# Two groups of x in one load, with rows of 32 KB into two slots side by side

## The chip, the cores and the metric

The kernel runs on one core of one Trainium2 chip. The metric is the device time of one execution in microseconds, the median of several runs. Times inside the kernel come from one profiled execution and count from the start of its span.

## The reference

The model is a factorization machine with a small network on top, for a batch of 1024 rows with 12,500 features each, all in float32. With x of shape 1024 x 12500, factors of 12500 x 16 and one linear weight per feature:

```
x_reg = x @ W_lin.T + b_lin
emb   = x @ factors                                    # 1024 x 16
sum_squared = square(emb.sum(axis=1))
squared_sum = (square(x) @ square(factors)).sum(axis=1)
h   = relu(emb @ W1.T + b1)                            # 16 -> 128
h   = relu(h @ W2.T + b2)                              # 128 -> 64
dnn = h @ W3.T + b3
y   = 0.5 + 5 * sigmoid(x_reg + 0.5 * (sum_squared - squared_sum) + dnn)
```

Nearly all of the data is x, 51.2 MB. Every element is read once, multiplied by 17 weights, and its square by one more.

## The kernel before

The host transposes x, so that features lie on the 128 partitions and the batch on the free axis. 12,500 features are one chunk of 128 (`xf`), a rest of 84 (`xl`), and 96 more chunks. The batch is worked in two halves of 512 columns. In a half, eight chunks make a group: 128 partitions x 8 chunks x 512 columns, 2 MB, in which each partition's row is 16 KB. There are 12 groups of the first half and 8 of the second; the last 32 chunks of the second half come apart, as ten "end pieces" of x that are cut by columns into a block of 384 and one of 128 (`PIECES`), so that the layers of the first block can run while the last loads still come.

**Ring.** `xr` has four slots (`RING`) of one group each, and so has `sq`, which takes the squares. SP issues all loads on one queue, in order: the weights (`hd`, L199), `xf`, `xl`, then groups 0 to 3 into slots 0 to 3 (L202, L203). In a loop (L205 to L211) it then waits for each slot until the group in it has been used (`sq_used`, L208) and loads the next group into it (L209). The end pieces follow in the same way (L213 to L217), each as soon as the slots that it covers are free.

**Who waits for a landing.** Each slot has its own semaphore, `x_landed[s]`. Three engines wait for it, each in its own order: ScalarE squares five chunks of the group in two instructions (L260 to L267), VectorE squares three (L346 to L350), TensorE multiplies.

**TensorE.** For every group, `multiply` (L440) adds 8 products of weights and x into the bank `p_lin` of the half, and `add_squares` (L446) adds 8 products of the squares, after waiting for VectorE and for ScalarE's first instruction, and before the last two for ScalarE's second. Each product shows as two records, so a group is two blocks of 16. All products are recorded on one line, L409. The last product of a group raises `sq_used` by one (L456). GpSimd sets out the weights of a group into `wr` and `wz` once the slot's last group has been used (`place`, L237).

**Between the halves.** After the 12 groups of the first half TensorE, ScalarE and VectorE run the layers of that half (L297 to L304, L359 to L362, L528 to L536), in the order of each engine's program, before any of them turns to the first group of the second half. The loads go on meanwhile, as far as slots are free. At the end the layers of the second half's two blocks are woven by hand between the end pieces (L543 to L579).

Of the kernel before, what the change touches and what calls it, by code (L numbers as in the profile page):

```python
# [14 lines left out]
P = 128  # L15
# [8 lines left out]
HALF = B // 2  # L24
CHUNKS = 8
RING = 4
ENDS = 32
ALL = (N - REST) // P
GROUPS = (ALL - 1) // CHUNKS
END_GROUPS = ENDS // CHUNKS  # L30
TOTAL = 2 * GROUPS - END_GROUPS
ROUNDS = (GROUPS // RING, (GROUPS - END_GROUPS) // RING)
W_END = ALL - ENDS

assert GROUPS % RING == 0 and (ALL - 1) % CHUNKS == 0 and END_GROUPS == RING


BY_DVE = 3
# [28 lines left out]
def fm_kernel(nc, head, x_first, x_rest, x_groups, x_end, out):  # L67
    with ExitStack() as ctx:
        def sb(name, shape, dt=F32):
            return ctx.enter_context(nc.sbuf_tensor(name, shape, dt))  # L70
# [4 lines left out]
        def sem(name):  # L75
            return ctx.enter_context(nc.semaphore(name))
# [3 lines left out]
        xl = sb("xl", [P, B])  # L80
        xr = sb("xr", [P, RING, CHUNKS, HALF])
        sqf = sb("sqf", [P, B])
        sql = sb("sql", [P, B])
        sq = sb("sq", [P, RING, CHUNKS, HALF])
        fsq = sb("fsq", [P, ALL, EMB])
        fsql = sb("fsql", [P, EMB])
        s_all = sb("s_all", [P, ALL])
        wr = sb("wr", [P, RING, CHUNKS, LIN])
        wz = sb("wz", [P, RING, CHUNKS, WZ])

        ws = sb("ws", [P, ENDS + 2, WZ])
        bias = sb("bias", [P, 1])
# [21 lines left out]
        hd_landed = sem("hd_landed")  # L114
        first_landed = sem("first_landed")
        rest_landed = sem("rest_landed")
        x_landed = [sem(f"x_landed{s}") for s in range(RING)]
        end_landed = [sem(f"end_landed{i}") for i in range(len(PIECES))]
        y_stored = sem("y_stored")
        zero_set = sem("zero_set")  # L120
# [11 lines left out]
        sq_used = sem("sq_used")  # L132
# [24 lines left out]
        def cols(k):  # L157

            c, n = BLOCKS[k]
            return slice(c, c + n)  # L160
# [6 lines left out]
        def row(k):  # L167

            c, n = BLOCKS[k]
            return slice(c // 2, (c + n) // 2)  # L170

        def tot_bank(k):
            return p_tot[k % 2]

        def width(i):
            return BLOCKS[PIECES[i][0]][1]

        def piece(a, i, c, n):

            at = ENDS * (BLOCKS[PIECES[i][0]][0] - HALF)  # L180
            return a[:, at + c * width(i):at + (c + n) * width(i)]
# [5 lines left out]
        def last_slot(i):  # L187
            k, c, n, _ = PIECES[i]
            return (ENDS * (BLOCKS[k][0] - HALF) + (c + n) * BLOCKS[k][1] - 1) // (CHUNKS * HALF)

# [6 lines left out]
        @block.sync  # L197
        def _(sp):
            sp.dma_start(hd[:, :], head).then_inc(hd_landed, 16)  # L199
            sp.dma_start(xf[:, :], x_first).then_inc(first_landed, 16)  # L200
            sp.dma_start(xl[0:REST, :], x_rest).then_inc(rest_landed, 16)  # L201
            for s in range(RING):  # L202
                sp.dma_start(xr[:, s].rearrange("p c b -> p (c b)"), x_groups[s]).then_inc(x_landed[s], 16)  # L203

            with sp.Fori(1, sum(ROUNDS)) as r:  # L205
                for s in range(RING):

                    sp.wait_ge(sq_used, RING * r + s + 1)  # L208
                    sp.dma_start(xr[:, s].rearrange("p c b -> p (c b)"),  # L209
                                 x_groups[bass.ds(RING * r + s, 1)].rearrange("g p n -> (g p) n")  # L210
                                 ).then_inc(x_landed[s], 16)  # L211
            at = 0
            for i, (k, c, n, _) in enumerate(PIECES):  # L213
                rows = x_end[at:at + P * n * width(i)].rearrange("(p m) -> p m", p=P)
                sp.wait_ge(sq_used, TOTAL + last_slot(i) + 1)
                sp.dma_start(piece(xe, i, c, n), rows).then_inc(end_landed[i], 16)
                at += P * n * width(i)  # L217

            for k in range(3):
                sp.wait_ge(y_ready[k], 1)  # L220
                sp.dma_start(out[cols(k)].rearrange("(u b) -> u b", u=2), y[64:P:32, row(k)]).then_inc(y_stored, 16)
            sp.wait_ge(y_stored, 48)

        @block.gpsimd
        def _(pool):
# [7 lines left out]
            nc.gpsimd.tensor_copy(ws[:, 0, LIN:WZ], s_all[:, 0:1]).then_inc(ws_ready, 1)  # L233
            nc.gpsimd.tensor_copy(ws[:, 1:ENDS + 1, LIN:WZ].rearrange("p c k -> p (c k)"),
                                  s_all[:, W_END:ALL]).then_inc(ws_ready, 1)
# [16 lines left out]
        @block.scalar  # L252
        def _(act):
            act.wait_ge(zero_set, 1)
            nc.scalar.activation(warm[:, :], zero[:, 0:1], ACT.Sigmoid)
            act.wait_ge(first_landed, 16)
            nc.scalar.activation(sqf[:, :], xf[:, :], ACT.Square).then_inc(first_squared, 1)  # L257

            def squares(r, s):
                act.wait_ge(x_landed[s], 16 * (r + 1))  # L260

                act.wait_ge(sq_used, RING * r + s + 1)
                c = BY_DVE
                for n in BY_ACT:
                    nc.scalar.activation(sq[:, s, c:c + n, :], xr[:, s, c:c + n, :],  # L265
                                         ACT.Square).then_inc(act_squared, 1)
                    c += n  # L267

            def square_end(i):
                k, c, n, m = PIECES[i]  # L270
                act.wait_ge(end_landed[i], 16)
                nc.scalar.activation(piece(sq_end, i, c, m), piece(xe, i, c, m),  # L272
                                     ACT.Square).then_inc(act_end_squared, 1)

            def copy_lin(k, u):
                nc.scalar.copy(lin[:, part(k, u)], p_lin[k][:, u * BLOCKS[k][1] // 2:(u + 1) * BLOCKS[k][1] // 2]  # L276
                               ).then_inc(lin_ready[k], 1)

            def layer1(k):
                act.wait_ge(p_h1_done[k], 1)  # L280
                nc.scalar.activation(h1[:, part(k, 0)], p_h1[0][:, 0:BLOCKS[k][1] // 2], ACT.Relu,
                                     bias=pr[:, C_B1:C_B1 + 1]).then_inc(h1a_ready[k], 1)

            def embedding_square(k):
                act.wait_ge(p_es_done[k], 1)
                nc.scalar.activation(gsq[0:64, row(k)], tot_bank(k)[0:64, row(k)], ACT.Square).then_inc(gsq_ready[k], 1)

            def sigmoid(k):
                act.wait_ge(p_tot_done[k], 1)
                nc.scalar.activation(sg[64:P, row(k)], tot_bank(k)[64:P, row(k)], ACT.Sigmoid,  # L290
                                     bias=bias[64:P, :]).then_inc(sg_ready[k], 1)

            with act.Fori(0, ROUNDS[0]) as r:
                for s in range(RING):
                    squares(r, s)

            act.wait_ge(sq_used, RING + GROUPS)  # L297
            copy_lin(0, 0)
            copy_lin(0, 1)
            layer1(0)  # L300
            act.wait_ge(pads_set, 3)
            embedding_square(0)
            act.wait_ge(bias_ready, 1)
            sigmoid(0)  # L304

            with act.Fori(ROUNDS[0], sum(ROUNDS)) as r:
                for s in range(RING):
                    squares(r, s)

            for i in range(6):  # L310
                square_end(i)
            act.wait_ge(p_lin_done[1], 1)
            copy_lin(1, 0)
            copy_lin(1, 1)
            layer1(1)
            nc.scalar.copy(rest[:, :], p_lin[1][:, BLOCKS[1][1]:HALF]).then_inc(rest_copied, 1)
            square_end(6)
            square_end(7)
            embedding_square(1)
            square_end(8)  # L320
            square_end(9)
            sigmoid(1)
            embedding_square(2)
            act.wait_ge(squares_done, 1)
            nc.scalar.copy(qs[:, :], p_sq[:, 0:P]).then_inc(qs_ready, 1)
            sigmoid(2)

        @block.vector
        def _(dve):
# [13 lines left out]
            nc.vector.tensor_tensor(sql[0:REST, :], xl[0:REST, :], xl[0:REST, :], ALU.mult).then_inc(rest_squared, 1)  # L343

            def squares(r, s):
                dve.wait_ge(x_landed[s], 16 * (r + 1))  # L346

                dve.wait_ge(sq_used, RING * r + s + 1)
                nc.vector.tensor_tensor(sq[:, s, 0:BY_DVE, :], xr[:, s, 0:BY_DVE, :], xr[:, s, 0:BY_DVE, :],  # L349
                                        ALU.mult).then_inc(dve_squared, 1)  # L350
# [56 lines left out]
        def _(pe):  # L407
# [30 lines left out]
                add_mm(quad(p_lin[h], 3, WZ, 0, HALF), ws[0:REST, ENDS + 1, :], sql[0:REST, half(h)])  # L438

            def multiply(r, s, h):  # L440
                pe.wait_ge(x_landed[s], 16 * (r + 1))
                pe.wait_ge(wr_ready, RING * r + s + 1)
                for c in range(CHUNKS):
                    add_mm(quad(p_lin[h], c, LIN, 0, HALF), wr[:, s, c, :], xr[:, s, c, :])
# [182 lines left out]
```

## Time and profile before

| what | us |
|---|---|
| median of three runs | 136.48 (136.37 to 136.83) |
| the profiled execution | 136.26 |
| its span, first to last instruction | 134.2 |
| TensorE busy | 105.3 |
| ScalarE busy | 64.2 |
| VectorE busy | 52.9 |
| GpSimd busy | 13.2 |
| bytes read | 52.16 MB |

Busy times are shares of one execution, and a matmul record's own time overlaps the next one's, so TensorE's busy time is longer than the work it stands for. The profile cuts the span into 40 slices and gives for each the rate of the loads in GB/s; its chain of waits goes back from the last instruction to what released each step. A landing is not a row of its own, but VectorE starts the squares of a group when it has landed, and the row says so ("<-DMA xr<-in_x_groups").

### The profile page before, as it was taken

Reading aid. Unit: us, or ns where it says so; the run is one execution under the profiler, and the core shown is the slowest. Engines: PE = TensorE matmul, PEld = TensorE weight load, DVE = VectorE, ACT = ScalarE, POOL = GpSimd, SP = SyncE. Lnnn points to the kernel's source line nnn. Section 1 sums busy time; section 2 is a strip of 40 time slices with the busy share of each in tenths; the row PEclk is TensorE's granted clock in tenths of the full one; section 3 lists DMA queues with packets and bytes.
Section 4 is the critical chain, followed back from the end, with each engine's and each line's share of the span. In section 5 each row is a group of like instructions: output and inputs, shape, how many; then the busy total and the mean of one; then the engine's idle time right before and its main releaser. Section 6 shows DMA issues by size and latency. Waiting matters only on the chain.

```text
span 134.2 us, 2683 instructions
## 1 busy us (share of the span) xinstructions
PE 105.3 (78%) x1034; PEld 28.9 (22%) x1034; DVE 52.9 (39%) x45; ACT 64.2 (48%) x67; POOL 13.2 (10%) x49
## 2 busy tenths in 40 slices
PE   6087966965976967967978969987887799779992
PEld 1022111110211111111112312211221122214780
DVE  0391451450550451352251393153254155557531
ACT  4030652560752662562473496373374374446741
POOL 5016011011011011011011001151000000000000
PEclk9999999999999999999999999999999999999999
DMA  4999999999999999999999999999999999999400
GB/s 129 406 385 435 415 440 420 435 425 420 430 430 430 420 440 420 440 410 445 415 440 420 440 420 435 415 440 420 440 415 435 401 440 429 412 397 409 180 5 1
DMA packets 4724, 52.25 MB, mean 389 GB/s; under 512 B 534, under 2 KB 666, under 8 KB 1646
## 3 DMA queue, kind: packets, MB, share of 16 engines
q1 hardware_dynamic: 4718, 52.16, 92.7%
q8 instruction: 5, 0.08, 0.3%
q14 instruction: 1, 0.01, 0.0%
HBM read 52.16 MB, written 0.00 MB: 389 GB/s over the span
## 4 chain that ended last, share of the span: by engine, by line
DMA 61%; PE 29%; DVE 3%; SPq 2%; issue 2%; ACT 1%; DVEq 0%; ACTq 0%
DMA xr<-in_x_groups 52%; PE p_lin L409 23%; DMA xr<-in_x_end 9%; PE p_tot L409 2%; PE p_h L480 2%; PE p_sq L409 1%; DVE sq L349 1%; DVE sq L355 1%; SPq L203 1%; PE p_h L504 1%; ACT sg L290 1%; SPq L201 0%; SPq L200 0%; SPq L199 0%; ACT lin L276 0%
## 5 line engine op out<-in xcount | busy, mean ns | idle before, releaser
L265 ACT ACTIVATE sq<-xr 128x1536 f32<-128x1536 f32 (+1 forms) x40 | 48.5, 1263 | 47.1 <-DMA xr<-in_x_groups 47.1
L349 DVE TENSOR_TENSOR sq<-xr 128x1536 f32<-128x1536 f32 x20 | 35.2, 1762 | 56.5 <-DMA xr<-in_x_groups 56.4
L409 PE MATMUL p_lin<-xr,wr 128*17 128x512 f32 x320 | 38.3, 595 | 16.4 <-DMA xr<-in_x_groups 16.4
L409 PE MATMUL p_lin<-sq,wz 128*18 128x512 f32 x320 | 38.4, 595 | 2.7 <-DVE sq L349 1.2
L409 PEld LDWEIGHTS p_lin<-xr,wr 128*17 128x17 f32 x320 | 8.1, 97 | 45.4 <-issue 23.0
L409 PEld LDWEIGHTS p_lin<-sq,wz 128*18 128x18 f32 x320 | 8.3, 97 | 32.4 <-ACT sq L265 19.5
L240 POOL COPY wr<-hd x20 | 5.9, 296 | 71.9 <-PE p_lin L409 71.4
L272 ACT ACTIVATE sq<-xr 128x1536 f32<-128x1536 f32 (+5 forms) x10 | 9.0, 929 | 7.6 <-DMA xr<-in_x_end 7.6
L355 DVE TENSOR_TENSOR sq<-xr 128x1536 f32<-128x1536 f32 (+3 forms) x8 | 9.2, 1156 | 7.8 <-DMA xr<-in_x_end 7.8
L409 PE MATMUL p_lin<-xr,hd 128*17 128x384 f32 (+1 forms) x128 | 8.9, 380 | 0.7 <-DMA xr<-in_x_end 0.7
L409 PE MATMUL p_lin<-sq,ws 128*18 128x384 f32 x64 | 5.9, 487 | 1.1 <-DVE sq L355 1.1
L409 PE MATMUL p_lin<-xf,hd 128*17 128x512 f32 x4 | 3.2, 961 | 3.7 <-DMA xf<-in_x_first 3.7
L242 POOL COPY wz<-s_all x20 | 5.4, 272 | 0.0
L409 PEld LDWEIGHTS p_lin<-xr,hd 128*17 128x17 f32 x128 | 3.9, 97 | 5.3 <-issue 2.7
L332 DVE SCALAR_TENSOR_TENSOR fsq<-hd 128x1552 f32<-128x1552 f32 x1 | 1.8, 1775 | 4.4 <-DMA hd<-in_head 4.4
L257 ACT ACTIVATE sqf<-xf 128x1024 f32<-128x1024 f32 x1 | 1.1, 1057 | 4.9 <-DMA xf<-in_x_first 4.9
L366 DVE TENSOR_SCALAR h<-p_h,hd 128x256 f32<-128x256 f32 (+2 forms) x3 | 1.3, 417 | 4.4 <-PE p_h L480 4.4
L409 PE MATMUL p_sq<-sq,ws 128*18 128x128 f32 x64 | 2.9, 273 | 0.0
L409 PEld LDWEIGHTS p_lin<-sq,ws 128*18 128x18 f32 x64 | 1.8, 97 | 5.0 <-ACT sq L272 3.4
L480 PE MATMUL p_h<-lin,hd 128*32 128x256 f32 (+2 forms) x40 | 2.4, 344 | 0.5 <-ACT lin L276 0.5
L409 PE MATMUL p_lin<-xl,hd 84*17 84x512 f32 x4 | 2.6, 780 | 0.0
L290 ACT ACTIVATE sg<-p_tot,bias 64x256 f32<-64x256 f32 (+2 forms) x3 | 1.2, 397 | 2.7 <-PE p_tot L409 2.7
(49 smaller groups left out, 34.2 us busy)
## 6 DMA issues: line engine op xcount, KB each, us to landing
xr<-in_x_groups SPq DMA_DIRECT2D x20, 2048.0 KB, 15.4
xr<-in_x_end SPq DMA_DIRECT2D x3, 1536.0 KB, 13.1
xr<-in_x_end SPq DMA_DIRECT2D x3, 512.0 KB, 13.0
xr<-in_x_end SPq DMA_DIRECT2D x1, 1152.0 KB, 14.3
hd<-in_head SPq DMA_DIRECT2D x1, 934.0 KB, 4.8
xr<-in_x_end SPq DMA_DIRECT2D x2, 384.0 KB, 14.5
xf<-in_x_first SPq DMA_DIRECT2D x1, 512.0 KB, 5.9
xl<-in_x_rest SPq DMA_DIRECT2D x1, 336.0 KB
```

Source lines behind the costliest of these rows:

```text
L203: sp.dma_start(xr[:, s].rearrange("p c b -> p (c b)"), x_groups[s]).then_inc(x_landed[s], 16)
L240: nc.gpsimd.tensor_copy(wr[:, bass.ds(s, 1), :, :].rearrange("p s c k -> p (s c) k"), w[:, bass.ds(at, CHUNKS), :]).then_inc(wr_ready, 1)
L242: nc.gpsimd.tensor_copy(wz[:, bass.ds(s, 1), :, LIN:WZ].rearrange("p s c k -> p (s c k)"), s_all[:, bass.ds(at, CHUNKS)]).then_inc(wz_read ...
L265: nc.scalar.activation(sq[:, s, c:c + n, :], xr[:, s, c:c + n, :], ACT.Square).then_inc(act_squared, 1)
L272: nc.scalar.activation(piece(sq_end, i, c, m), piece(xe, i, c, m), ACT.Square).then_inc(act_end_squared, 1)
L290: nc.scalar.activation(sg[64:P, row(k)], tot_bank(k)[64:P, row(k)], ACT.Sigmoid, bias=bias[64:P, :]).then_inc(sg_ready[k], 1)
L332: nc.vector.scalar_tensor_tensor(fsq[:, :, :], w[:, :, 0:EMB], -0.5, w[:, :, 0:EMB], ALU.mult, ALU.mult).then_inc(fsq_ready, 1)
L349: nc.vector.tensor_tensor(sq[:, s, 0:BY_DVE, :], xr[:, s, 0:BY_DVE, :], xr[:, s, 0:BY_DVE, :], ALU.mult).then_inc(dve_squared, 1)
L355: nc.vector.tensor_tensor(piece(sq_end, i, c + m, n - m), piece(xe, i, c + m, n - m), piece(xe, i, c + m, n - m), ALU.mult).then_inc(dve_e ...
L409: return nc.tensor.matmul(out, lhsT, rhs, start=False, stop=False, skip_group_check=True)
L480: mm = nc.tensor.matmul(bank[32 * t:32 * t + 32, 0:n], pr[:, C_W1 + 32 * t:C_W1 + 32 * t + 32], rhs, start=True, stop=True, skip_group_che ...
L504: mm = nc.tensor.matmul(p_h2[32 * t:32 * t + 32, row(k)], pr[:, C_W2 + t % 2 * 32:C_W2 + t % 2 * 32 + 32], h1[:, part(k, t // 2)], start=T ...
```

## The change

Groups are loaded in pairs. The host lays two groups that follow each other side by side, so that each partition has one row of 32 KB for both. A transfer brings such a pair, 4 MB, into two neighbouring slots of the ring: slots 0 and 1, or slots 2 and 3. There are two landing semaphores instead of four, one for each pair of slots. SP waits until both groups of a pair of slots have been used and then issues one load. Slots, squares, products, their order on every engine, and the end pieces stay as they were.

```diff
+TWO = 2
...
-        x_landed = [sem(f"x_landed{s}") for s in range(RING)]
+        x_landed = [sem(f"x_landed{t}") for t in range(RING // TWO)]
...
-            for s in range(RING):
-                sp.dma_start(xr[:, s].rearrange("p c b -> p (c b)"), x_groups[s]).then_inc(x_landed[s], 16)
+            for t in range(RING // TWO):
+                sp.dma_start(xr[:, TWO * t:TWO * t + TWO].rearrange("p s c b -> p (s c b)"),
+                             x_groups[t]).then_inc(x_landed[t], 16)
 
             with sp.Fori(1, sum(ROUNDS)) as r:
-                for s in range(RING):
-
-                    sp.wait_ge(sq_used, RING * r + s + 1)
-                    sp.dma_start(xr[:, s].rearrange("p c b -> p (c b)"),
-                                 x_groups[bass.ds(RING * r + s, 1)].rearrange("g p n -> (g p) n")
-                                 ).then_inc(x_landed[s], 16)
+                for t in range(RING // TWO):
+
+                    sp.wait_ge(sq_used, RING * r + TWO * t + TWO)
+                    sp.dma_start(xr[:, TWO * t:TWO * t + TWO].rearrange("p s c b -> p (s c b)"),
+                                 x_groups[bass.ds(RING // TWO * r + t, 1)].rearrange("g p n -> (g p) n")
+                                 ).then_inc(x_landed[t], 16)
...
-                act.wait_ge(x_landed[s], 16 * (r + 1))
+                act.wait_ge(x_landed[s // TWO], 16 * (r + 1))
...
-                dve.wait_ge(x_landed[s], 16 * (r + 1))
+                dve.wait_ge(x_landed[s // TWO], 16 * (r + 1))
...
-                pe.wait_ge(x_landed[s], 16 * (r + 1))
+                pe.wait_ge(x_landed[s // TWO], 16 * (r + 1))
...
-    x_groups = np.empty((TOTAL, P, CHUNKS * HALF), f32)
+    x_groups = np.empty((TOTAL // TWO, P, TWO, CHUNKS * HALF), f32)
     for g in range(TOTAL):
         h, c = g // GROUPS, CHUNKS * (g % GROUPS)
-        x_groups[g] = chunks[c:c + CHUNKS, :, h * HALF:(h + 1) * HALF].transpose(1, 0, 2).reshape(P, -1)
+        x_groups[g // TWO, :, g % TWO] = chunks[c:c + CHUNKS, :, h * HALF:(h + 1) * HALF].transpose(1, 0, 2).reshape(P, -1)
+    x_groups = x_groups.reshape(TOTAL // TWO, P, TWO * CHUNKS * HALF)
```

## Rows read from the trace of the kernel before

**Rows 1.** The page: span, load rate in 40 slices, last chain by line.
```profile
span 134.2 us, 2683 instructions
...
GB/s 129 406 385 435 415 440 420 435 425 420 430 430 430 420 440 420 440 410 445 415 440 420 440 420 435 415 440 420 440 415 435 401 440 429 412 397 409 180 5 1
...
DMA xr<-in_x_groups 52%; PE p_lin L409 23%; DMA xr<-in_x_end 9%; PE p_tot L409 2%; PE p_h L480 2%; PE p_sq L409 1%; DVE sq L349 1%; DVE sq L355 1%; SPq L203 1%; PE p_h L504 1%; ACT sg L290 1%; SPq L201 0%; SPq L200 0%; SPq L199 0%; ACT lin L276 0%
```

**Rows 2.** Timeline of VectorE: start, duration in us, instruction, count, idle before and releaser.
```profile
5.58 1.77 DVE L332 SCALAR_TENSOR_TENSOR fsq<-hd 128x1552 f32<-128x1552 f32 x1 [4.44 <-DMA hd<-in_head]
...
18.19 1.76 DVE L349 TENSOR_TENSOR sq<-xr 128x1536 f32<-128x1536 f32 x1 [3.15 <-DMA xr<-in_x_groups]
...
27.96 1.76 DVE L349 TENSOR_TENSOR sq<-xr 128x1536 f32<-128x1536 f32 x1 [3.13 <-DMA xr<-in_x_groups]
33.59 1.76 DVE L349 TENSOR_TENSOR sq<-xr 128x1536 f32<-128x1536 f32 x1 [3.87 <-DMA xr<-in_x_groups]
...
67.84 1.76 DVE L349 TENSOR_TENSOR sq<-xr 128x1536 f32<-128x1536 f32 x1 [3.13 <-DMA xr<-in_x_groups]
...
87.94 1.84 DVE L349 TENSOR_TENSOR sq<-xr 128x1536 f32<-128x1536 f32 x1 [3.64 <-DMA xr<-in_x_groups]
...
107.52 1.76 DVE L349 TENSOR_TENSOR sq<-xr 128x1536 f32<-128x1536 f32 x1 [3.13 <-DMA xr<-in_x_groups]
...
123.57 0.69 DVE L355 TENSOR_TENSOR sq<-xr 128x512 f32<-128x512 f32 x1 [0.41 <-DMA xr<-in_x_end]
124.86 0.69 DVE L355 TENSOR_TENSOR sq<-xr 128x512 f32<-128x512 f32 x1 [0.59 <-DMA xr<-in_x_end]
```

**Rows 3.** Timeline of TensorE, from group 13 to the end pieces.
```profile
80.51 1.91 PE L409 MATMUL p_lin<-xr,wr 128*17 128x512 f32 x16
82.22 1.91 PE L409 MATMUL p_lin<-sq,wz 128*18 128x512 f32 x16
...
107.52 1.91 PE L409 MATMUL p_lin<-xr,wr 128*17 128x512 f32 x16 [0.99 <-DMA xr<-in_x_groups]
109.52 1.91 PE L409 MATMUL p_lin<-sq,wz 128*18 128x512 f32 x16
111.24 1.49 PE L409 MATMUL p_lin<-xr,hd 128*17 128x384 f32 x16
...
120.47 1.49 PE L409 MATMUL p_lin<-sq,ws 128*18 128x384 f32 x16 [0.40 <-DVE sq L355]
121.76 1.49 PE L409 MATMUL p_lin<-xr,hd 128*17 128x384 f32 x16
```

**Rows 4.** Timeline of SP's issues: head, two refills, the last store.
```profile
0.75 0.39 SPq L199 DMA_DIRECT2D hd<-in_head  x1
...
71.95 0.33 SPq L209 DMA_DIRECT2D xr<-in_x_groups  x1
...
84.32 0.33 SPq L209 DMA_DIRECT2D xr<-in_x_groups  x1
...
132.29 0.47 SPq L221 DMA_DIRECT2D out_y<-y  x1
```

**Rows 5.** Windows: length, busy us of each engine, clock, DMA share, GB/s.
```profile
0.75:1.50 0.75, 0.30 (x1) 0.13 (x2) 0.27 (x1) 0.75 (x1) 0.75 (x2) 1.00 0.00 0
```

**Rows 6.** Timeline of TensorE's first products.
```profile
7.22 1.86 PE L409 MATMUL p_lin<-xf,hd 128*17 128x512 f32 x2 [3.71 <-DMA xf<-in_x_first]
...
8.88 1.06 PE L409 MATMUL p_lin<-xf,hd 128*17 128x512 f32 x1
...
10.61 0.60 PE L409 MATMUL p_lin<-sqf,ws 128*18 128x512 f32 x1
...
12.01 0.59 PE L409 MATMUL p_lin<-sql,ws 84*18 84x512 f32 x1
```

**Rows 7.** Waits: who waited for whom, us in total, times, longest.
```profile
PE p_lin L409 <- DMA xr<-in_x_groups: 16.4, 17, 1.7
```

**Rows 8.** The chain of waits where the second half begins: start, us, what.
```profile
76.78 1.77 DVE sq L349
```

More of the change, by code:

```diff
@@ L33 @@
 W_END = ALL - ENDS
-assert GROUPS % RING == 0 and (ALL - 1) % CHUNKS == 0 and END_GROUPS == RING
+assert RING % TWO == 0 and GROUPS % RING == 0 and (ALL - 1) % CHUNKS == 0 and END_GROUPS == RING
 BY_DVE = 3
```

## The prediction

> **What bounds the kernel now.** I read the page first, then the landings, then what releases a slot. On the page [rows 1] the reader is to see a kernel bound by its loads: the slices move 400 to 445 GB/s from the second to the 37th, and the chain that ended last is 52% loads of x in the first 20 groups, 9% loads of the last 32 chunks, 23% matmuls. VectorE begins the squares of a group as soon as it has landed, so its starts mark the landings [rows 2]. Between 33.59 and 67.84 seven groups land, one every 4.89 us: (67.84 - 33.59)/7. TensorE needs less than that. With work in hand it starts a block of 16 matmul records (the x half or the squares half of one group) every 1.71 us (80.51 to 82.22), so a group takes it 3.43 us; from an idle start the squares hold it up once, by 2.00 instead of 1.71 (107.52 to 109.52) [rows 3]. So TensorE idles about 1 us per group, and the queue is never empty: a slot is asked for again about 4.1 us after its group has landed (67.84 to 71.95, group 11) [rows 2, 4], while three other groups, 14.7 us of transfer, are still queued. That reserve is what the change spends.
>
> Below, "group" counts from 0 and "landing" is the start of the squares. Pair p holds groups 2p and 2p+1; before, its second group lands last, so I compare with the landings of groups 1, 3, 11, 15 and 19.
>
> **The transfers themselves (a gain).** Ten transfers of 4 MB take the place of 20 of 2 MB. What one costs beyond its bytes follows from two sizes in a full queue: 2048 KB in 4.89 us, 512 KB in 1.29 us (123.57 to 124.86) [rows 2]. The slope is 3.60 us for 1536 KB, so 2048 KB of bytes are 4.80 us and 0.09 us belong to the transfer and its 128 rows. Halving transfers and rows saves 0.09 per pair: X = 9.78 - 0.09 = 9.69 us, 0.9 us over ten pairs. No row shows 32 KB rows. The lower bound is no gain (rows cut in two by the queue); the upper bound is the best slice, 445 GB/s [rows 1], by which 4.19 MB take 9.43 us. I take 9.69, next to the measured sizes. SP issues ten fewer transfers, 0.33 us each for those in the loop [rows 4], in time in which it otherwise waits for a slot: nothing.
>
> By the Trainium skill, DMA: Bandwidth & Descriptors, section "Anatomy of one DMA", a transfer costs some 2.0 us plus its bytes at 436 GB/s (a fit for another issue path). Paid in a row, that would make ten fewer transfers worth 20 us. The rows contradict it for a full queue: 2048 KB would take 6.8 us and take 4.89.
>
> **The turn of a pair (a loss of reserve).** Both slots are now released together, so after a landing TensorE does two groups before the refill is issued: 4.11 (one group, 67.84 to 71.95) plus 3.43 = 7.54 us [rows 2 to 4]. In that time only one other pair, 9.69 us, feeds the queue. The refill must reach the engines in time. An issue on an empty queue costs F beyond its bytes. The only such load is the first: head is issued at 0.75, seen at 5.58, and its 934 KB are worth 934/2048 x 4.89 = 2.23 us, so F = 2.60 [rows 2, 4]. From below: no byte moves between 0.75 and 1.50 [rows 5], so F is at least 0.75. In between: the last store of 0.5 KB, issued at 132.29, ends with the span at 134.2, 1.9 us [rows 1, 4]. I take F = 2.0, since the first load of the program also has the first read in it. The rule for each pair is then: landing = the later of (landing of the pair before + X) and (issue + F + X). Steady state: 7.54 + 2.0 = 9.54 against 9.69: just no stall. At F = 2.6 there is one of 0.45 us in every second pair.
>
> **First pair.** Group 0 alone no longer starts the work; pair 0 lands at 18.19 - 0.09 = 18.10 instead of 13.28. The lost start is itself hidden, since the loads go on. But TensorE, which ended its first matmuls at 12.6 (12.01 + 0.59), stands still for 5.5 us [rows 6]. Since its clock rose it had never stood longer than 1.7 us for a landing [rows 7]. Rows 6 show what a pause does at the start: after the clearing matmuls it waited 3.71 us, and the first products then took 1.06 us a record where the same shape later takes 0.60, the lower level (1.2 GHz) against the upper (2.4 GHz). (The clock column reads 1.00 even at the start [rows 5], so I go by the durations.) It ran 2.7 us (7.22 to about 9.9) before it was on the upper level. I expect pair 0 to start on the lower level and to lose half of such a stretch, 1.35 us. Bounds: 0 (the clock holds) and 6.8 us (all four blocks of both groups at half speed, 4 x 1.71 more). Then: issue at 18.10 + 7.54 + 1.35 = 26.99, landing of pair 2 at 26.99 + 2.0 + 9.69 = 38.68; without a stall 18.10 + 2 x 9.69 = 37.48. Cost 1.20 us, on the path, since everything behind is loads. After that the gaps are some 2.5 us (9.69 less two groups' 7.2), nearer to the 1.7 that the clock outlasted, and I cost them at nothing. (The extra 0.74 us before 33.59 is in the old trace and I leave it in both.)
>
> The Trainium skill has this rule in TensorE: Matmul & The Clock Gate, section "HAM oscillation — how this bites in real kernels": bursts of matmuls with a wait for loads between them can fall back to the lower clock each time. The trace shows no fall in gaps up to 1.7 us, so for the shorter waits the measurement stands against it; at the long first gap the page and rows 6 point the same way.
>
> **The middle, where half 0 ends.** After group 11 TensorE, ScalarE and VectorE do the layers of the first half; VectorE is back at squares at 76.78 [rows 8]. Before, that delay ate reserve only: the slot of group 13 was reissued at 84.32 [rows 4], with two more groups still on their way. Now (without the first stall) pair 5 lands at 67.84 - 6 x 0.09 = 67.30, its refill is issued at 74.84, 2.89 us later than group 11's at 71.95, and the layers and groups 12 and 13 follow 2.89 later: refill at 84.32 + 2.89 = 87.21. Pair 7, the last one queued, lands at 87.94 - 8 x 0.09 = 87.22. So pair 8 lands not at 87.22 + 9.69 = 96.91 but at 87.21 + 2.0 + 9.69 = 98.90, a stall of 1.99 us. Pair 9 (issued around 95, in time) lands at 108.59; group 19 landed at 107.52. Net +1.07: stall 1.99, less 0.92 saved.
>
> **The end.** Groups 18 and 19 now reach TensorE together, and it has no gap left before the end. From a landing: 3.72 for group 18 (107.52 to 111.24), 3.43 for group 19, four blocks of 1.29 for the end pieces 0 and 1 (120.47 to 121.76), and 1.29 for the x half of piece 2 [rows 3]: the squares of piece 2 start 13.60 after the landing, at 122.19, where they started at 120.47: +1.72. VectorE's 1.76 us per square and the last loads, which move by +1.07, are both earlier than that. From 120.47 on TensorE had work without a gap, so the rest moves as a whole.
>
> **Sum** against the profiled execution (136.26 us; span 134.2): +1.72 and +1.20, 139.18. The median of the runs, 136.48, lies 0.22 higher, so 139.4.
>
> **Rivals.**
> - A, the sum above: 139.4. Chance 0.42.
> - B, the clock holds in the first gap: the first refill at 25.64 is in time (25.64 + 11.69 = 37.33 before 37.48), and only the middle costs: 138.2. For it: the upper level never fell in 120 us of the old trace; against it: no gap there was half as long. 0.25.
> - C, an empty queue costs F = 2.6 each time: 0.6 more in the middle and 0.45 at pairs 2, 4 and 6, thus 140.2 with the clock up, 141.5 with A's slow first pair. For it: the only measured load from empty; against it: that one also opens the program. 0.17.
> - D, the other side: long rows stream so much faster that they pay for the stalls. Each 0.1 us less of X brings the end forward by about 0.8. With B's clock it decides at X = 9.47 (443 GB/s); at 9.43, the best slice, it gives 138.2 - 2.1 = 136.1. Against it: the stretch between 33.59 and 67.84 runs at 429 and the fitted cost of 0.09 leaves no more to save. 0.08.
> - E, rows cut in two, so the change saves nothing: A plus about 0.7, 140.1. 0.08.
>
> Range: 137.6 (B with F = 1.4) to 141.6 (C at its worse end), which leaves out D and little else. A measurement of this kernel can tell about 0.3%, 0.4 us, from no change; D splits evenly between faster and same, so faster 0.04, same 0.04, slower 0.92.
>
> **What would show it.** Right: landings 9.7 us apart in pairs, two groups back to back on TensorE and a gap of about 2.5 us; a first landing near 18.1; products of pair 0 at some 1 us a record at first; a hole in the load rate near 28 and one near 88 to 89; pair 9 near 109.8 (108.6 without the first stall); TensorE without gaps from there on. Wrong: no hole near 88 (then the release in the middle came earlier than I place it), holes in every pair (C), pair 0 at 0.60 us a record (B), pairs closer than 9.6 us (D) or 9.8 apart with as many packets as before (E).

## The result, and the profile after

The changed kernel takes 147.71 us (median of four runs, 147.31 to 149.29) against 136.55 before: 1.084 times as long (95% interval 1.080 to 1.087). Forecast was 139.4. The direction was right and the size was not: 11.2 us lost, 2.9 expected. Times and ratios, here and below, leave out executions that took over 1.5% longer than the fastest of the same kernel.

The page after, with lines that answer to [rows 1]: the span, the granted clock of TensorE in tenths and the load rate, each in 40 slices; the last chain; and its line on the loads (count, KB each, us from issue to landing).
```profile
span 145.2 us, 2649 instructions
...
PEclk9999857999659999959999999968959999999999
...
GB/s 154 433 367 433 433 433 433 131 406 433 433 433 433 244 361 433 433 433 433 289 388 433 406 433 433 221 424 433 289 397 433 380 435 261 387 396 417 235 5 1
...
DMA xr<-in_x_groups 51%; PE p_lin L412 41%; PE p_sq L412 1%; PE p_tot L412 1%; PE p_h L483 1%; SPq L203 0%; SPq L202 0%; SPq L201 0%; PE p_h L507 0%; ACT sg L293 0%; SPq L212 0%; ACT gsq L289 0%; DVE y L379 0%
...
xr<-in_x_groups SPq DMA_DIRECT2D x10, 4096.0 KB, 14.3
```
The chain that ended last has 41% matmuls where it had 23%: the loads now wait for TensorE's work. In undisturbed slices the loads run at 433 GB/s, a little better than before. But the row has a hole every third to sixth slice (131, 244, 289, 221, 289, 261), and the clock falls beside several of them. The landings show the holes, VectorE's timeline as in [rows 2]:
```profile
18.17 3.43 DVE L352 TENSOR_TENSOR sq<-xr 128x1536 f32<-128x1536 f32 x2 [7.66 <-DMA xr<-in_x_groups]
27.87 3.52 DVE L352 TENSOR_TENSOR sq<-xr 128x1536 f32<-128x1536 f32 x2 [6.28 <-DMA xr<-in_x_groups]
40.55 3.43 DVE L352 TENSOR_TENSOR sq<-xr 128x1536 f32<-128x1536 f32 x2 [9.16 <-DMA xr<-in_x_groups]
50.25 3.43 DVE L352 TENSOR_TENSOR sq<-xr 128x1536 f32<-128x1536 f32 x2 [6.27 <-DMA xr<-in_x_groups]
62.08 3.43 DVE L352 TENSOR_TENSOR sq<-xr 128x1536 f32<-128x1536 f32 x2 [8.40 <-DMA xr<-in_x_groups]
71.78 3.43 DVE L352 TENSOR_TENSOR sq<-xr 128x1536 f32<-128x1536 f32 x2 [6.27 <-DMA xr<-in_x_groups]
...
84.15 3.43 DVE L352 TENSOR_TENSOR sq<-xr 128x1536 f32<-128x1536 f32 x2
94.13 3.43 DVE L352 TENSOR_TENSOR sq<-xr 128x1536 f32<-128x1536 f32 x2 [6.55 <-DMA xr<-in_x_groups]
105.42 3.43 DVE L352 TENSOR_TENSOR sq<-xr 128x1536 f32<-128x1536 f32 x2 [7.87 <-DMA xr<-in_x_groups]
117.94 3.43 DVE L352 TENSOR_TENSOR sq<-xr 128x1536 f32<-128x1536 f32 x2 [9.09 <-DMA xr<-in_x_groups]
```
These are pairs 0 to 9. Undisturbed, a pair takes 9.70 us (18.17 to 27.87, 40.55 to 50.25, 62.08 to 71.78); forecast 9.69. Every other interval is longer: pair 2 by 2.98, pair 4 by 2.13, pairs 6 and 7 together by 2.95 (71.78 to 94.13; pair 6's row shows the layers' end, not its landing), pair 8 by 1.59, pair 9 by 2.82: 12.5 us. SP's issues of pairs 2, 4 and 9 show how late they were asked for:
```profile
28.20 0.35 SPq L212 DMA_DIRECT2D xr<-in_x_groups  x1
...
49.64 0.33 SPq L212 DMA_DIRECT2D xr<-in_x_groups  x1
...
103.10 0.33 SPq L212 DMA_DIRECT2D xr<-in_x_groups  x1
```
Call the time from a refill's issue to the landing of the pair ahead of it what is *left*. Pair 2 was issued with nothing left (28.20, pair 1 landed at 27.87), pair 4 with 0.61, pair 9 with 2.32 (pair 8 landed at 105.42) and still lost 2.82. Pairs 3 and 5, issued at 35.42 and 57.80 with 5.13 and 4.28 left, lost nothing.

TensorE's timeline of pair 0, the counterpart of [rows 3], and the windows (length, busy us of each engine, clock, loads) over the starts of pairs 0, 2 and 4:
```profile
18.17 3.62 PE L412 MATMUL p_lin<-xr,wr 128*17 128x512 f32 x16 [5.58 <-DMA xr<-in_x_groups]
21.56 2.99 PE L412 MATMUL p_lin<-sq,wz 128*18 128x512 f32 x16
24.37 1.89 PE L412 MATMUL p_lin<-xr,wr 128*17 128x512 f32 x16
26.09 1.89 PE L412 MATMUL p_lin<-sq,wz 128*18 128x512 f32 x16
```
```profile
18.00:24.00 6.00, 5.83 (x32) 1.28 (x36) 3.43 (x2) 4.75 (x4) 0.00 (x0) 0.52 1.00 431
40.00:44.00 4.00, 3.44 (x20) 0.74 (x24) 3.43 (x2) 3.46 (x3) 0.00 (x0) 0.50 0.95 410
62.00:65.00 3.00, 2.92 (x16) 0.68 (x20) 2.92 (x2) 2.93 (x3) 0.00 (x0) 0.55 1.07 459
```
After the idle 5.58 us the clock is at its lower level (0.52 over the stretch): the first two blocks take 3.39 and 2.81 us from start to next start, instead of 1.72. The same is seen behind the holes ahead of pairs 2 and 4. So two suspects stand side by side: late refills, and a clock that falls in the holes and makes the next refill later.

The packets of the loads add a third. A pair is 128 packets of 32 KB, one for each row, on 16 DMA engines, and 16 packets of 4 bytes, one behind the last row of each engine; I take these as the ends of the engines' shares. The line on packets, for six stretches of the changed kernel's trace: 102.90 to 103.65 and 104.75 to 105.10 (ends of pair 8), 104.05 to 104.75 and 106.65 to 106.98 (first rows of pair 9), 114.20 to 115.10 and 115.10 to 117.60 (ends of pair 9, among rows of the end pieces):
```profile
DMA packets 15, 0.00 MB, mean 0 GB/s; under 512 B 15, under 2 KB 15, under 8 KB 15
DMA packets 1, 0.00 MB, mean 0 GB/s; under 512 B 1, under 2 KB 1, under 8 KB 1
...
DMA packets 15, 0.49 MB, mean 702 GB/s; under 512 B 0, under 2 KB 0, under 8 KB 0
DMA packets 1, 0.03 MB, mean 99 GB/s; under 512 B 0, under 2 KB 0, under 8 KB 0
...
DMA packets 40, 0.33 MB, mean 364 GB/s; under 512 B 15, under 2 KB 15, under 8 KB 15
DMA packets 85, 1.05 MB, mean 421 GB/s; under 512 B 1, under 2 KB 1, under 8 KB 1
```
Fifteen engines had ended pair 8 by 103.62 and the last at 105.04; fifteen began pair 9 between 104.07 and 104.73, some 1.0 us and more after its issue, and the last at 106.89. That engine ended pair 9 at 117.49, the others by 115.08. The landing is the last engine's: when the refill of pair 9 was issued with 2.32 us left, fifteen of sixteen had at most some 0.5 us of work.

### The profile page after: what moved, and what is told of

It is laid out like the page before. It is cut to its first block, busy times and chain, and to the rows that moved or that the text cites. A ratio compares the mean times of both kernels' runs of the same rounds, so it can differ in the third digit from the quotient of the medians.

```text
span 145.2 us, 2649 instructions
## 1 busy us (share of the span) xinstructions
PE 109.2 (75%) x1034; PEld 32.0 (22%) x1034; DVE 52.1 (36%) x45; ACT 63.1 (43%) x67; POOL 14.4 (10%) x49
## 4 chain that ended last, share of the span: by engine, by line
DMA 51%; PE 45%; issue 1%; SPq 1%; ACT 0%; DVE 0%
DMA xr<-in_x_groups 51%; PE p_lin L412 41%; PE p_sq L412 1%; PE p_tot L412 1%; PE p_h L483 1%; SPq L203 0%; SPq L202 0%; SPq L201 0%; PE p_h L507 0%; ACT sg L293 0%; SPq L212 0%; ACT gsq L289 0%; DVE y L379 0%
## 5 line engine op out<-in xcount | busy, mean ns | idle before, releaser
L268 ACT ACTIVATE sq<-xr 128x1536 f32<-128x1536 f32 (+1 forms) x40 | 47.5, 1259 | 59.7 <-DMA xr<-in_x_groups 59.7
L412 PE MATMUL p_lin<-xr,wr 128*17 128x512 f32 x320 | 44.8, 684 | 26.5 <-DMA xr<-in_x_groups 26.5
L352 DVE TENSOR_TENSOR sq<-xr 128x1536 f32<-128x1536 f32 x20 | 34.4, 1760 | 67.6 <-DMA xr<-in_x_groups 67.5
L412 PE MATMUL p_lin<-sq,wz 128*18 128x512 f32 x320 | 40.8, 629 | 1.5 <-DVE sq L352 1.2
L412 PEld LDWEIGHTS p_lin<-xr,wr 128*17 128x17 f32 x320 | 9.2, 104 | 56.7 <-issue 52.6
L412 PEld LDWEIGHTS p_lin<-sq,wz 128*18 128x18 f32 x320 | 9.9, 106 | 32.3 <-issue 21.9
L243 POOL COPY wr<-hd x20 | 7.1, 356 | 81.7 <-PE p_lin L412 81.2
L279 ACT COPY lin<-p_lin 128x256 f32<-128x256 f32 (+1 forms) x4 | 1.2, 349 | 3.1 <-PE p_lin L412 3.1
```

What stands on the lines that cost most here:

```text
L243: nc.gpsimd.tensor_copy(wr[:, bass.ds(s, 1), :, :].rearrange("p s c k -> p (s c) k"), w[:, bass.ds(at, CHUNKS), :]).then_inc(wr_ready, 1)
L412: return nc.tensor.matmul(out, lhsT, rhs, start=False, stop=False, skip_group_check=True)
```

## The experiments

The theories: 1, the loss feeds itself through the clock, since an issue on an empty queue costs some 2.7 us and one made earlier than that costs nothing; 2, it is the loads' own (long rows, restart of an empty queue); 3, landing or release in pairs is enough by itself; 4, formed after the first four runs below (six spare products, the two halves of the change, rows of 16 KB), a refill needs far more time in hand than 2.7 us. Times stand beside runs of the kernel before on the same chip, 136.45 to 136.66 us.

**Spare work for TensorE, so that the clock holds.** Nothing else changes:
```diff
+            idle_work(16)      # spare bf16 products of 512 columns into p_h1[0]
...
+                    if s % TWO == 0:
+                        idle_work(6)
                     multiply(r, s, 0)
```


> The changed kernel with idle work for TensorE: 16 spare products of 512 columns into a bank that is free (1.2 GHz or 2.4 GHz, nothing reads them) ahead of the first pair, and six ahead of every pair, so that no pause is long enough for the clock to fall. Theory 1 (the refill is too late by a little, and each hole lets the clock fall, which makes the next refill later still): every pair is released 7.5 us after its landing instead of up to 10.0, holes of about 0.5 us at pairs 2, 4 and 6 and 2.7 us in the middle remain, 139.5 us (139 to 141). Theory 2 (the loss is the loads' own, in the restart of an empty queue or in rows of 32 KB): no change, 147 to 148 us.

147.96 and 149.84 us, ratio 1.089 (1.081 to 1.098): theory 1's 139.5 is refuted as far as six products held the clock. They did not hold it everywhere (mean 0.962), so a second run has twelve.

> As the run with idle work for TensorE, but with twelve spare products ahead of every pair instead of six (2.6 us), so that the clock has no pause to fall in even behind a hole. Theory 1 (late by the clock's falls): 139.5 us (139 to 142). Theory 4 (a refill has to be issued some 4.5 us before the pair ahead of it has landed, since an engine of the queue that has run empty restarts late, each at another time, and the landing waits for the last of 16; at the release 7.5 us after a landing only 2.2 us are left, so it is late with the clock up as well): 146 to 150 us, with 10.5 to 12.5 us between landings.

147.61 us, ratio 1.079 (1.076 to 1.082). The mean granted clock, VectorE's timeline of pairs 1 to 3 and SP's issues of pairs 2 and 3:
```profile
core 0: 145.6 us, clock 1.000
```
```profile
28.94 3.43 DVE L352 TENSOR_TENSOR sq<-xr 128x1536 f32<-128x1536 f32 x2 [7.46 <-DMA xr<-in_x_groups]
38.99 3.43 DVE L352 TENSOR_TENSOR sq<-xr 128x1536 f32<-128x1536 f32 x2 [6.62 <-DMA xr<-in_x_groups]
51.54 3.43 DVE L352 TENSOR_TENSOR sq<-xr 128x1536 f32<-128x1536 f32 x2 [9.13 <-DMA xr<-in_x_groups]
```
```profile
25.85 0.35 SPq L212 DMA_DIRECT2D xr<-in_x_groups  x1
36.49 0.34 SPq L212 DMA_DIRECT2D xr<-in_x_groups  x1
```
The clock stands at 1.000, yet pair 3, issued at 36.49 with 2.50 us left before pair 2's landing at 38.99, came 2.85 us late (51.54 - 38.99 - 9.70). Pair 2, with 3.09 left, lost 0.35. The falls of the clock go along with the loss, but the loss is there without them. By the packets fifteen engines had ended pair 3 by 48.60, and the last at 51.10.

Pair 1 came 1.2 us late in this run, with its load queued from the start. There too one engine ended late: fifteen by 27.22, the last at 28.34 (stretches 26.20 to 27.30 and 27.30 to 28.50). The third line, for 25.55 to 25.60, shows a packet of 16 KB of the queue that the page calls "instruction"; it starts at 25.57 and takes 1.02 us:
```profile
DMA packets 26, 0.36 MB, mean 328 GB/s; under 512 B 15, under 2 KB 15, under 8 KB 15
DMA packets 7, 0.20 MB, mean 164 GB/s; under 512 B 1, under 2 KB 1, under 8 KB 1
...
q8 instruction: 1, 0.02, 127.2%
```
A row of x that starts as it ends (26.57) takes 1.76 us instead of 1.22. The kernel before has such packets at 29.02 and 82.72, and its landings at 33.59 and 87.94 are 0.74 and 0.51 us late; the changed kernel has one at 90.89, ahead of the late pair 7. That these packets held up the engine is read from the times; no run took them out.

**One half of the change at a time.** The kernel before, with the release in pairs alone, and with the landing in pairs alone:
```diff
-                    sp.wait_ge(sq_used, RING * r + s + 1)
+                    if s % 2 == 0:
+                        sp.wait_ge(sq_used, RING * r + s + 2)
```
```diff
-                pe.wait_ge(x_landed[s], 16 * (r + 1))        # ScalarE and VectorE alike
+                pe.wait_ge(x_landed[s // 2], 32 * (r + 1))
```


> The kernel before with the release in pairs alone: SP waits until both slots of a pair are used and then issues their two loads of 2 MB back to back; four landing semaphores, so each group is still worked as it lands. Theory 1 (it is landing and release in pairs together that use up the reserve): at the second group's landing another 9.8 us of loads are queued and the refill is there after 4.1 + 2.7 = 6.8 us, so nothing is lost: 136.5 us, within 0.4. Theory 3 (the release in pairs alone empties the queue): 140 us or more.

> The kernel before with the landing in pairs alone: loads of 2 MB into single slots, each slot released by itself, but two slots share one landing semaphore and all engines wait for both. Theory 1: the first group's refill is issued 4.1 us after the pair's landing and the second's at 7.5, with 9.8 us of loads queued, so the queue never empties; the clock may fall in the first gap of 5.5 us; only the end is later, two groups there in a row: 137.2 us (136.6 to 138). Theory 3 (the work in pairs, with its pauses and falls of the clock, is enough by itself): 140 us or more.

Release alone: 136.84 us, ratio 1.003 (1.001 to 1.006). Landing alone: 137.40, 1.009 (1.005 to 1.013). Theory 3 falls. With the landing in pairs alone, VectorE's timeline of two pairs and the issues between them:
```profile
48.53 3.43 DVE L349 TENSOR_TENSOR sq<-xr 128x1536 f32<-128x1536 f32 x2 [6.36 <-DMA xr<-in_x_groups]
58.33 3.43 DVE L349 TENSOR_TENSOR sq<-xr 128x1536 f32<-128x1536 f32 x2 [6.37 <-DMA xr<-in_x_groups]
```
```profile
42.86 0.33 SPq L209 DMA_DIRECT2D xr<-in_x_groups  x1
46.28 0.33 SPq L209 DMA_DIRECT2D xr<-in_x_groups  x1
```
The first slot's refill is asked for with 5.67 us left, the second's then queues behind it, and the landings keep 9.80 us. The clock fell here as well (mean 0.949), and cost little.

**Both halves, but rows of 16 KB** (two loads of 2 MB in place of one of 4 MB; the two edits above together).

> Landing and release both in pairs, but two loads of 2 MB with rows of 16 KB in place of one of 4 MB. Theory 1: as the changed kernel, plus 0.09 us for each of the ten pairs: 148 to 149 us. Theory 2, as far as it blames the rows of 32 KB: back near 136.5 to 139 us.

148.97 and 148.99 us, where theory 1 had 148 to 149. The long rows are not to blame.

**The slots released earlier.** The changed kernel, whole; TensorE takes both groups' x products first, and raises a new semaphore once all squares are there:
```diff
-                    sp.wait_ge(sq_used, RING * r + TWO * t + TWO)
+                    sp.wait_ge(x_used, RING * r + TWO * t + TWO)
...
                     multiply(r, s, 0)
+                    multiply(r, s + 1, 0)
                     add_squares(r, s, 0)
+                    add_squares(r, s + 1, 0)     # its first product raises x_used by TWO
```


> The changed kernel, whole, with the slots released earlier: TensorE does the x half of both groups first, and a new semaphore releases the pair when the x products of both are done and ScalarE and VectorE have squared both, before the squares of the second group are multiplied; some 5.5 us after the landing instead of 7.5, so that 4.2 us are left. Theory 1 (2.7 us are enough when the clock is up): holes only behind the first pair and in the middle, 139 us (138 to 140). Theory 4 (4.5 us needed): most of the loss goes, but some 0.5 us at other pairs too, 141 us (139.5 to 143). If it stays at 146 or more, the time of the release is not the cause.

> The changed kernel, whole, with the early release (after both groups' x products and squares) and with twelve spare products ahead of every pair, ten more ahead of the first, so that the clock stays up: pairs released 5.4 us after the landing every time, 4.3 us ahead of need. Theory 4 (some 4.5 us needed, whatever the clock; the clock mattered only where it moved the release): small losses at pairs and one of 1 to 2 us in the middle, 139.5 us (138.5 to 141.5). If the pairs lose as much as in the run with the early release alone (145 us), the clock is not what was left there.

144.10 (of two executions) and, with spare work as well, 144.65 us (1.06 times as long as before). Some 3 to 3.5 us come back. Both expectations missed, theory 4's too: it had 139.5 to 143 and 138.5 to 141.5. In the second run, with 3.2 to 4.8 us left at a release, the pairs lose 0 to 1.5 us each, and in the middle, with 1.35 left (issue 89.71, landing ahead 91.06), 2.66.

**The transfers by themselves.** Both kernels with most of the square half of the 20 groups left out (VectorE squares one chunk, ScalarE two, one product of squares) and with spare work.

> The kernel before with most of the square half of the 20 groups left out (one chunk squared by VectorE and one chunk in each of ScalarE's two instructions, one product of squares per group), with six spare products for TensorE every second group to hold its clock: the loads as they are, slots free 3 us after a landing. Base for the next run: bound by the loads, 136 us (135.5 to 136.6).

> The changed kernel with the same part left out and 16 spare products ahead of every pair: pairs released some 4.2 us after the landing, 5.5 us ahead of need. What the larger transfers are worth by themselves. By the fitted 0.09 us for each pair: 0.9 us below the run before it, less 0.6 at the end for two groups in a row, so 0.3 us (0 to 0.9) faster. Theory 2 as far as it blames the rows of 32 KB: slower by 3 us or more. Theory 4: no holes, at most one of 1 us in the middle.

136.44 and 137.98 us (ratios to the whole kernel before: 0.999, 0.997 to 1.000, and 1.014, 1.008 to 1.020). I had expected the second 0.3 us faster than the first; it was 1.5 slower. Pairs are 9.71 us apart where undisturbed, so the saving per pair is real, but with 4.2 us left most of the time the pairs lose up to 0.7, and the middle 1.3; the change still doesn't pay.

**Late refills without pairs.** The kernel before, most of the square half left out, SP asking for a slot two groups later; in the second run six of eight x products are left out too:
```diff
-                    sp.wait_ge(sq_used, RING * r + s + 1)
+                    sp.wait_ge(sq_used, RING * r + s + 3)
```


> The kernel before, loads of 2 MB with rows of 16 KB, each group landing by itself, with most of the square half left out as in the base run (136.4 us); SP asks for a slot only when the group two later has been used, so that each refill is issued about 3.0 us after a landing with 1.8 us of loads left. No pairs, no rows of 32 KB, little work. Theory 1 (a refill costs 2.6 us from an empty queue and nothing if issued earlier than that): 0.75 us lost for every two loads, 142 us (140 to 143.5). Theory 4 (some 4.5 us needed): 1.5 to 2.5 us for every two loads, 148 to 156 us. Theory 2 as far as it blames the landing in pairs or the long rows: 136.5 us.

> As the run with the refills asked for two groups late, with six of the eight x products left out as well, so that the refill is issued 1.3 us after a landing with 3.5 us of loads left. Theory 1 (2.6 us are enough): nothing lost, 136.4 us (136 to 137). Theory 4: 0.5 to 1.5 us for every two loads, 140 to 148 us.

163.62 us (ratio 1.198, 1.194 to 1.201) and 158.91 (1.168, 1.160 to 1.176). Both are above what theory 4 named. In the first the products ran slower than I had assumed (mean clock 0.83), so at most 0.3 us were left, and each second load lost 3.4 to 4.0. The second has the fewest other changes in its way; VectorE's timeline of groups 3 to 9, and SP's issues of groups 4 to 9:
```profile
28.00 0.69 DVE L349 TENSOR_TENSOR sq<-xr 128x512 f32<-128x512 f32 x1 [4.19 <-DMA xr<-in_x_groups]
34.90 0.69 DVE L349 TENSOR_TENSOR sq<-xr 128x512 f32<-128x512 f32 x1 [6.21 <-DMA xr<-in_x_groups]
41.37 0.69 DVE L349 TENSOR_TENSOR sq<-xr 128x512 f32<-128x512 f32 x1 [5.77 <-DMA xr<-in_x_groups]
47.83 0.69 DVE L349 TENSOR_TENSOR sq<-xr 128x512 f32<-128x512 f32 x1 [5.76 <-DMA xr<-in_x_groups]
53.85 0.69 DVE L349 TENSOR_TENSOR sq<-xr 128x512 f32<-128x512 f32 x1 [5.33 <-DMA xr<-in_x_groups]
61.23 0.69 DVE L349 TENSOR_TENSOR sq<-xr 128x512 f32<-128x512 f32 x1 [6.69 <-DMA xr<-in_x_groups]
66.41 0.69 DVE L349 TENSOR_TENSOR sq<-xr 128x512 f32<-128x512 f32 x1 [4.48 <-DMA xr<-in_x_groups]
```
```profile
26.38 0.35 SPq L209 DMA_DIRECT2D xr<-in_x_groups  x1
31.21 0.34 SPq L209 DMA_DIRECT2D xr<-in_x_groups  x1
38.06 0.33 SPq L209 DMA_DIRECT2D xr<-in_x_groups  x1
44.62 0.33 SPq L209 DMA_DIRECT2D xr<-in_x_groups  x1
51.09 0.33 SPq L209 DMA_DIRECT2D xr<-in_x_groups  x1
57.11 0.33 SPq L209 DMA_DIRECT2D xr<-in_x_groups  x1
```
What was left at the issue, and what the load lost against 4.89 us:

| group | 4 | 5 | 6 | 7 | 8 | 9 |
|---|---|---|---|---|---|---|
| left | 1.62 | 3.69 | 3.31 | 3.21 | 2.76 | 4.12 |
| lost | 2.01 | 1.58 | 1.57 | 1.13 | 2.49 | 0.29 |

Group 4: left 28.00 - 26.38, lost 34.90 - 28.00 - 4.89. No pair, no long row, hardly any work: under 3 us in hand cost 2.0 to 2.5, some 3.5 cost 1.1 to 1.6, over 4 cost 0.3. A fixed price of 2.7 us, counted from the landing ahead, would have made five of these six cost nothing. Here too the landing waits for the last engine: of groups 0 to 3, loaded in a row, the sixteen ends lie 0.9 us apart, of groups 4 to 9 1.7 to 3.2. This trace has no packet of the "instruction" queue before 88.64, so there the engines part without one.

The figure is no constant. In the run with the landing in pairs alone, group 4 was issued at 24.99, 3.2 us before group 3 was in, and lost nothing: its sixteen ends, 31.79 to 32.64, are 4.9 us behind those of group 3 (26.83 to 27.73).

**The changed kernel again,** beside the last three runs.

> The changed kernel once more, unaltered, to be timed on the same chip as the three runs below: 147.7 us (147 to 149.5).

148.65 us, ratio 1.090 (1.087 to 1.092).

## Why the prediction was wrong

**The step that failed** is the rule of the turn: "landing = the later of (landing of the pair before + X) and (issue + F + X)", with F = 2.0 and the reading "9.54 against 9.69: just no stall". From an empty queue F was 2.65 (28.20 to 40.55, less 9.70) and 2.74 for pair 4, what the first load had shown (2.60) and I had marked down. With 2.7 and the issues as they came, the rule gives pairs 2 and 4 at 40.60 and 62.04; they landed at 40.55 and 62.08. It still fails for pairs 8 and 9, which it has at 104.10 and 115.50: they landed at 105.42 and 117.94. What it lacks is that a landing waits for the last of 16 engines. Fifteen had ended these pairs by 103.62 and 115.08, and a landing is seen 0.4 us behind the last end (117.49 to 117.94), so fifteen engines kept the rule and one was 1.4 and 2.4 us behind. Counted from the landing ahead, a refill with over 4 us left lost at most 0.7 us in nearly all cases, one with 2.3 to 3.7 between nothing and 2.9; I had 2.15 (9.69 - 7.54) and called it enough. That turns the steady state from no loss to one of 2 to 3 us at pairs 2 and 4, part of it the clock's (below). Rival C had the place right and at 140.2 to 141.5 the size wrong: it had F = 2.6, but neither the later falls of the clock nor the late engine.

**The clock at the first gap** fell as forecast, and cost more: pair 0 was released 10.03 us after its landing instead of 8.89, 2.49 for the clock where I took 1.35. That it would hold afterwards, a term that I put at nothing, was wrong too: pauses of 5.33, 4.49, 2.64 and 2.53 us ahead of pairs 2, 4, 7 and 8 had a clock of 0.50, 0.55, 0.68 and 0.61 behind them (one of 3.76 ahead of pair 9 had 1.00). Pairs 2 and 4 were released 9.09 and 8.56 us after their landings instead of 7.54. By the Trainium skill, TensorE: Matmul & The Clock Gate, section "HAM oscillation — how this bites in real kernels", a wait for loads between bursts can lower the clock at each burst; the trace agrees (0.50 and 0.55 at pairs 2 and 4). But holding it at 1.000 brought the time only to 147.61, against 147.71 and 148.65 without: up to 1 us, inside the spread between the two.

**The transfers:** X = 9.69 forecast, 9.70 measured; right. The Trainium skill, DMA: Bandwidth & Descriptors, section "Rules for kernel authors", asks for 1 MiB or more per transfer for full rate; the kernel before had twice that, and the trace agrees that little was left to gain (429 to 432 GB/s: 2 MB in 4.89 us, 4 MB in 9.70).

**The middle:** forecast a stall of 1.99 at pair 8; pair 8 lost 1.59, after a release 7.55 us after VectorE's return from the layers (84.15 to 91.70). The size is close in part by luck. I had the refill issued with nothing left (87.21 against 87.22); it had 2.43, by which the rule, even with F = 2.7, has only 0.27 of stall. Pair 7's landing was itself late by one engine (fifteen ends by 92.82, the last at 93.54); the typical engine ran out at 92.0, 0.3 us after the issue, so the refill was late for most engines, as forecast.

**The end:** forecast 13.60 us from pair 9's landing to the squares of piece 2; they start at 131.55, 13.61 after 117.94. Right.

**Sum:** pair 9 landed 10.42 later than group 19 [rows 2]: 12.47 lost in holes, less 0.72 saved in nine pairs, less 1.3 that the old landings had lost themselves (0.74 and 0.51 of it beside the "instruction" packets; the prediction left the 0.74 in both). The end adds 0.66, and the span grew by 11.0. (Of the slices that I read as 400 to 445 GB/s, two are lower, 385 and 397; nothing hangs on them.)

What stays open is why the engines part. The packets show that they do, behind late refills and beside "instruction" packets, and that the late engine of pair 9 stood idle from 105.04 to 106.89 with its refill issued at 103.10. The Trainium skill, same page on DMA, section "Latency and other measured facts", says that the fixed cost is smaller under lighter HBM load; 2.65 to 2.74 us from a queue that had run out against 3.6 to 5.3 from issue to landing, less the bytes, in the second late-refill run would fit, but the first of the two, with 0.3 us left, cost 3.9 to 4.1, so that nothing here settles it. A ring of three pairs, which would give long rows their reserve, was not tried; the most that it could win is the 0.9 us of the transfers.

## What to carry to other kernels

In a kernel bound by its loads, ask first how many us of loads are still queued when a refill is issued, and measure how much the queue wants: here, counted from the landing ahead, over 4 us to be safe in most cases, more than the 2.7 of an issue from an empty queue. A landing is the last engine's; look at when the others end, since they run dry first. Merging two loads halves the number of refills in flight as well as their overhead; with a ring of the same size it turned 10.6 us in hand (14.7 less 4.1) into some 2 and lost 8%. Each half of the merge (one landing, one release) was nearly free (0.9% and 0.3%); together they took one group's work and one group's load out of the reserve at once.

## What was not expected of the hardware

A load issued while 2 to 3 us of others were still queued, by the landing ahead, landed up to 2.8 us later than its bytes explain, in pairs and in single loads alike. In pairs 8 and 9, and in pair 3 with spare work, most of that was one engine of sixteen that ended 1.4 to 2.5 us behind the rest. And a clock held at 1.000 for a whole kernel, its pauses filled by spare products, bought next to nothing: in that trace too single engines ended late (pair 3: fifteen by 48.60, the last at 51.10).
